# One conditioned attention block on one core: projections spread over the head slots, q and k side by side in one stack, six transfers per half stack in place of nine

## What is computed

```python
ln = (h - mu) / jnp.sqrt(var + EPS) * ln_g + ln_b
gamma = (w @ Wg.T + bg)[:, None, :]
beta = (w @ Wb.T + bb)[:, None, :]
# h = gamma * ln + beta
qkv = (h @ Wqkv.T + bqkv).reshape(B, N, num_heads, hd, 3)
energy = jnp.einsum('bhqd,bhkd->bhqk', q, k)
att = jax.nn.softmax(energy, axis=-1) / D ** 0.5
out = jnp.einsum('bhqk,bhkd->bhqd', att, v)
out = out @ Wp.T + bp
h1 = out + hidden
h2 = _sln(h1, w, ln_g, ln_b, Wg, bg, Wb, bb)
# result: h2 + h1
```

## Time and profile before

| what | value |
|---|---|
| median of 3 runs | 434.63 us (433.49 to 435.28) |
| profiled execution | 434.07 us |
| its span on the core, first to last instruction | 432.3 us |
| granted TensorE clock, mean | 0.963 |
| TensorE matmul busy | 376.3 us, 87% |
| VectorE busy | 316.9 us, 73% |
| ScalarE busy | 247.4 us, 57% |
| GpSimd busy | 44.4 us, 10% |
| DMA | 53.69 MB, mean 124 GB/s |

### The profile page before, as it was taken

One profiled execution on the slowest core, in us unless ns is written; L12 is line 12 of the kernel. 1 busy time (PEld: TensorE's weight loads), 2 busy tenths in 40 slices (PEclk: granted clock), 3 DMA queues, 4 the chain that ended last, 5 costly groups with the idle time before them and its releaser, 6 DMA issues.

```text
span 432.3 us, 9025 instructions
## 1 busy us (share of the span) xinstructions
PE 376.3 (87%) x3240; PEld 307.0 (71%) x3241; DVE 316.9 (73%) x777; ACT 247.4 (57%) x453; POOL 44.4 (10%) x46
## 2 busy tenths in 40 slices
PE   4958598899898999999998999898999999988972
PEld 4627496788686878877786878777877778766652
DVE  7617566669686887879797878787787978685644
ACT  7421247556474756566565757575656656664650
POOL 5000000002010100102020101010010201010111
PEclk9987779999899999999999999999999999999996
DMA  6198887878759668989697988779897978493021
GB/s 192 38 117 107 123 103 116 160 109 137 123 127 131 144 124 157 127 143 148 118 159 121 155 116 161 126 156 125 146 127 133 142 106 163 77 186 96 7 71 49
DMA packets 50367, 53.69 MB, mean 124 GB/s; under 512 B 6642, under 2 KB 41857, under 8 KB 50322
## 3 DMA queue, kind: packets, MB, share of 16 engines
q1 hardware_dynamic: 50322, 53.11, 73.6%
HBM read 14.18 MB, written 4.23 MB: 43 GB/s over the span
## 4 chain that ended last, share of the span: by engine, by line
PE 55%; DMA 14%; SPq 12%; issue 7%; DVE 7%; ACT 3%; POOL 0%; POOLq 0%; DVEq 0%; ACTq 0%
PE m L669 20%; DMA kst<-qk_l 14%; PE st L669 11%; PE sa L669 10%; SPq L286 10%; PE pv L669 10%; DVE mx L458 3%; PE pv L759 2%; SPq L289 2%; ACT p L436 2%; PE m L833 1%; ACT hT L424 1%; DVE qst L615 1%; DVE qk_l L492 1%; DVE m_l L467 1%
## 5 line engine op out<-in xcount | busy, mean ns | idle before, releaser
L458 DVE TENSOR_REDUCE mx<-sa 128x2 f32<-128x512 f32 x256 | 174.4, 683 | 93.5 <-PE sa L669 93.3
L436 ACT ACTIVATE p<-st 128x512 f32<-128x512 f32 x256 | 150.3, 598 | 78.3 <-PE st L669 75.0
L669 PE MATMUL sa<-kst,qst 128*128 128x256 f32 x512 | 109.8, 298 | 15.9 <-DMA kst<-qk_l 14.7
L669 PE MATMUL st<-qst,kst 128*128 128x256 f32 x512 | 111.4, 301 | 4.9 <-ACT p L436 4.9
L669 PEld LDWEIGHTS sa<-kst,qst 128*128 128x128 f32 x512 | 82.0, 198 | 21.7 <-DMA kst<-qk_l 13.3
L669 PEld LDWEIGHTS st<-qst,kst 128*128 128x128 f32 x512 | 79.4, 193 | 16.6 <-ACT p L436 9.4
L669 PE MATMUL pv<-p,v_st 128*32 128x256 f32 x1024 | 68.7, 386 | 0.7 <-ACT p L436 0.7
L349 POOL TENSOR_TENSOR h1b<-h,gb 128x512 f32<-128x512 f32 x16 | 20.4, 1277 | 250.4 <-DVE h L548 250.4
L669 PEld LDWEIGHTS pv<-p,v_st 128*32 128x32 f32 x1024 | 26.8, 109 | 20.5 <-ACT p L436 0.9
L669 PE MATMUL m<-hT_h,wqkv_h 128*128 128x256 f32 x128 | 39.0, 305 | 0.0
L669 PE MATMUL m<-hT_l,wqkv_h 128*128 128x256 f32 x128 | 37.5, 293 | 0.0
(11 more groups left out here) (97 smaller groups left out, 529.7 us busy)
## 6 DMA issues: line engine op xcount, KB each, us to landing
qst<-qk_h SPq DMA_DIRECT2D x64, 128.0 KB
qst<-qk_l SPq DMA_DIRECT2D x64, 128.0 KB
kst<-qk_h SPq DMA_DIRECT2D x64, 128.0 KB
kst<-qk_l SPq DMA_DIRECT2D x64, 128.0 KB
xa<-x_dram SPq DMA_DIRECT2D x16, 256.0 KB, 4.1
xd<-x_dram SPq DMA_DIRECT2D x16, 256.0 KB, 4.5
gb<-gb_rows SPq DMA_DIRECT2D x16, 256.0 KB, 4.5
out_dram<-y SPq DMA_DIRECT2D x16, 256.0 KB, 4.3
```

Source lines behind the costliest of these rows:

```text
L436: nc.scalar.activation(p32[:, h % PR, :], st_ps[h % 2][:], ACT.Exp).then_inc(exp_done, 1)
L458: dve.tensor_reduce(mx[:, par(a), h // HH, (h % HH) * TT:(h % HH + 1) * TT], sa_ps[h % 2][:].rearrange("p (t n) -> p t n", t=TT), AX.X, AL ...
L669: return nc.tensor.matmul(o, l, r, start=start, stop=stop)
```

## The change

- q and k lie side by side: `qk` holds for each half and part (high, low) q and then k, and one stack `qkst` of 67 rows has for each head q's 256 columns and then k's 256. Rows 0-15 (high of both) and 48-63 (low of both) are filled by one transfer of 256 KiB each, the others by four of 128 KiB. Six transfers for nine. The two whole halves wait for q's and k's low parts together.
- Row 64 is zero for q and stays so; `scores_max` multiplies only rows 0 to 64, `scores` all 67. So the rows of the maxima need no clearing, and no pad rows exist; the four large memsets at the start go.
- The projections' slots are lists: q in slots 0, 1, 3, 4, k in 1, 3, 4, 5, v in 7, 7, 8, 9, output in 11, 12, 13, 15. The transposes of x move from slot 13 to 11, the attention transposes to bank pv1, the maxima to pv0 (slot 1) and pv1 (slot 10), each with two transposes, since a maxima tile now has 8 rows of 256.
- h's high part is made from h in SBUF by one instruction, two slots after the transposes of x; its low part, the normalised x, and the bias of the output (now added to x before the residual, not by two matmuls) are GpSimd's.
- The table of VectorE follows; `residual` begins one step later.

```diff
-ROWS = 4 * HD + 2
+ZERO_ROW = 4 * HD
+ROWS = ZERO_ROW + 3
 VC = 2 * HD
 LAG = 3
 LEAD = 1
 PR = 8
 
-S_MT1, S_Q, S_K, S_MT0, S_AT, S_V, S_P, S_XT = 1, 2, 3, 7, 8, 8, 10, 13
+Q_SLOTS, K_SLOTS, V_SLOTS, P_SLOTS = (0, 1, 3, 4), (1, 3, 4, 5), (7, 7, 8, 9), (11, 12, 13, 15)
+S_MT1, S_AT, S_MT0, S_XT = 1, 8, 10, 11
+S_QH, S_KH, S_VH = 5, 6, 10
 WARM = 14
-NSTK = 9
+NSTK = 6
 S_O1, S_O0 = 3, 11
+S_OT1, S_OT0 = 5, 13
...
-        qk_h = sb("qk_h", [P, 2, 2, 2, N], F32R)
-        qk_l = sb("qk_l", [P, 2, 2, 2, N], F32R)
-        qst = sb("qst", [P, 2, H, N], F32R)
-        kst = sb("kst", [P, 2, H, N], F32R)
+        qk = sb("qk", [P, 2, 2, 2, 2, N], F32R)
+        qkst = sb("qkst", [ROWS, 2, H, 2, N], F32R)
         v_st = sb("v_st", [P, 2, TT, H, VC])
-        mx = sb("mx", [P, 2, 2, P])
-        m_h = sb("m_h", [HH * TT, 2, P], F32R)
-        m_l = sb("m_l", [HH * TT, 2, P], F32R)
+        mx = sb("mx", [P, 2, 2, TT, P])
+        m_h = sb("m_h", [HH, 2, N], F32R)
+        m_l = sb("m_l", [HH, 2, N], F32R)
...
+            for r in range(ZERO_ROW, ROWS):
+                sp.dma_start(raw(qkst[r:r + 1, :, :, 1, :]).rearrange("a p h n -> a (p h) n"),
+                             ones[0:2 * H, :]).then_inc(fixed_rows_in, 16)
+            sp.dma_start(raw(qkst[ZERO_ROW:ZERO_ROW + 1, :, :, 0, :]).rearrange("a p h n -> a (p h) n"),
+                         zrows[:]).then_inc(fixed_rows_in, 16)
...
-            def stack(a, g, t):
-
-                if not has(a):
-                    return
-                if first(a):
-                    sp.wait_ge(pad_v_zero, 1)
+            def stack(a, g):
+
+                if not has(a):
+                    return
                 wait(sp, st_done, 16 * (a - 2) + HH * (g + 1))
-                wait(sp, (ql_ready, kl_ready)[t], 1 * a + 1)
+                wait(sp, ql_ready, 1 * a + 1)
+                wait(sp, kl_ready, 1 * a + 1)
                 s, p = stack_in[g][par(a)], par(a)
-                dst, hi, lo = (qst, kst)[t], qk_h[:, p, t, g, :], qk_l[:, p, t, g, :]
-                for r, src in enumerate((hi, lo, hi, lo) if t == 0 else (hi, hi, lo, lo)):
-                    sp.dma_start(raw(dst[r * HD:(r + 1) * HD, p, g * HH:(g + 1) * HH, :]),
+
+                def part(r, t, src):
+                    sp.dma_start(raw(qkst[r * HD:(r + 1) * HD, p, g * HH:(g + 1) * HH, t, :]),
                                  raw(src)).then_inc(s, 16)
-                if t == 0:
-                    sp.dma_start(raw(qst[4 * HD:ROWS, p, g * HH:(g + 1) * HH, :]), zrows[:]).then_inc(s, 16)
+
+                for r, e in ((0, 0), (3, 1)):
+                    part(r, slice(0, 2), qk[:, p, g, e])
+                part(1, 0, qk[:, p, g, 1, 0])
+                part(1, 1, qk[:, p, g, 0, 1])
+                part(2, 0, qk[:, p, g, 0, 0])
+                part(2, 1, qk[:, p, g, 1, 1])
...
             def step(b):
-                stack(b + 1, 1, 0)
-                stack(b + 1, 1, 1)
+                stack(b + 1, 1)
                 maxima(b, 1)
                 if has(b + 4):
                     wait(sp, xn_ready, 1 * (b + 2) + 1)
                     sp.dma_start(xa[:, par(b + 4)], x_t[b + 4]).then_inc(x_in[par(b + 4)], 16)
-                stack(b + 2, 0, 0)
+                stack(b + 2, 0)
                 maxima(b + 1, 0)
-                stack(b + 2, 0, 1)
...
+            def norm_x(a):
+
+                wait(pool, rstd_ready, 1 * a + 1)
+                wait(pool, xnT_done, 1 * a)
+                for t in range(TT):
+                    o = pool.tensor_scalar(xn[:, t, :], xa[:, par(a), t, :], mv[:, t, 0:1], rstd[:, 0, t:t + 1],
+                                           ALU.subtract, ALU.mult)
+                o.then_inc(xn_ready, 1)
+
+            def add_bias(a):
+
+                if first(a):
+                    pool.wait_ge(bias_ready, 1)
+                wait(pool, xd_in[par(a)], 32 * (half(a) + 1))
+                pool.tensor_tensor(xd[:, par(a)], xd[:, par(a)],
+                                   bias_b[:].rearrange("p (a n) -> p a n", a=1).broadcast_to([P, TT, D]),
+                                   ALU.add).then_inc(xdb_ready, 1)
+
+            def low_h(a):
+
+                if not has(a):
+                    return
+                wait(pool, hTh_ready, 1 * a + 1)
+                pool.tensor_tensor(hT_l[:, par(a)], hT[:], hT_h[:, par(a)], ALU.subtract).then_inc(hTl_ready, 1)
+
...
+                    if h == 5 and has(b + 3) and not first(b + 3):
+                        norm_x(b + 3)
+                    if h == 9 and has(b - 1):
+                        add_bias(b - 1)
+                    if h == 13:
+                        low_h(b + 3)
...
-            def high_h(a, k):
-
-                if not has(a):
-                    return
-                wait(act, xnT_done, 1 * a + 1)
+            def high_h(a):
+
+                if not has(a):
+                    return
+                wait(act, hT_ready, 1 * a + 1)
                 wait(act, v_done, 1 * (a - 2) + 1)
-                nc.scalar.activation(hT_h[:, par(a), k, :], m0[:, k * N:(k + 1) * N], ACT.Identity,
-                                     bias=bcol[:, k:k + 1], scale=gcol[:, k:k + 1]).then_inc(hTh_ready, 1)
+                nc.scalar.activation(hT_h[:, par(a)], hT[:], ACT.Copy).then_inc(hTh_ready, 1)
...
-                    if h == S_Q + 4 and has(b + 2):
+                    if h == S_QH and has(b + 2):
...
-                    if h == S_K + 4 and has(b + 2):
+                    if h == S_KH and has(b + 2):
...
-                    if h == S_V + 4 and has(b + 1):
+                    if h == S_VH and has(b + 1):
...
-                    if h == 15:
-                        high_h(b + 3, 0)
-                        high_h(b + 3, 1)
+                    if h == S_XT + 2:
+                        high_h(b + 3)
...
-            act.wait_ge(consts_ready, 1)
-            for pad in (kst, qst):
-                nc.scalar.activation(pad[:, 1].rearrange("p h n -> p (h n)"),
-                                     ones[:, 0:1].broadcast_to([P, H * N]), ACT.Copy, scale=0.0).then_inc(pad_1_zero, 1)
...
-                dve.tensor_reduce(mx[:, par(a), h // HH, (h % HH) * TT:(h % HH + 1) * TT],
+                dve.tensor_reduce(mx[:, par(a), h // HH, :, h % HH],
...
-                    wait(dve, xd_in[par(a)], 32 * (half(a) + 1))
+                    wait(dve, xdb_ready, 1 * a + 1)
...
                 between = {
-                    (0, 0): [lambda: residual(b - 2, 2)],
-                    (0, 1): [lambda: low_h(b + 2), lambda: residual(b - 2, 3)],
-                    (2, 0): [lambda: norm1(b + 3, 0), lambda: low_max(b, 1)],
-                    (2, 1): [lambda: norm1(b + 3, 1)],
-                    (4, 0): [lambda: residual(b - 2, 4), lambda: norm1(b + 3, 2)],
-                    (5, 0): [lambda: normalise(b - 1, 1, 0)],
-                    (5, 1): [lambda: normalise(b - 1, 1, 1)],
-                    (6, 1): [lambda: low_qk(b + 2, 0, m0, qh_ready, ql_ready)],
-                    (7, 1): [lambda: low_qk(b + 2, 1, m1, kh_ready, kl_ready)],
-                    (8, 1): [lambda: low_max(b + 1, 0), lambda: residual(b - 2, 5)],
+                    (0, 0): [lambda: residual(b - 2, 0)],
+                    (1, 0): [lambda: residual(b - 2, 1)],
+                    (2, 0): [lambda: residual(b - 2, 2)],
+                    (2, 1): [lambda: low_max(b, 1)],
+                    (3, 0): [lambda: residual(b - 2, 3), lambda: norm1(b + 3, 0)],
+                    (3, 1): [lambda: norm1(b + 3, 1)],
+                    (4, 1): [lambda: norm1(b + 3, 2)],
+                    (5, 1): [lambda: low_qk(b + 2, 0, m0, qh_ready, ql_ready)],
+                    (6, 0): [lambda: normalise(b - 1, 1, 0)],
+                    (6, 1): [lambda: low_qk(b + 2, 1, m1, kh_ready, kl_ready)],
+                    (7, 0): [lambda: normalise(b - 1, 1, 1)],
+                    (8, 1): [lambda: residual(b - 2, 4)],
                     (9, 1): [lambda: low_att(b - 1)],
-                    (11, 0): [lambda: norm1(b + 3, 3)],
-                    (11, 1): [lambda: norm1(b + 3, 4)],
-                    (13, 0): [lambda: normalise(b, 0, 0)],
-                    (13, 1): [lambda: normalise(b, 0, 1)],
-                    (14, 1): [lambda: residual(b - 1, 0)],
-                    (15, 0): [lambda: residual(b - 1, 1)],
+                    (10, 1): [lambda: residual(b - 2, 5), lambda: norm1(b + 3, 4)],
+                    (11, 1): [lambda: low_max(b + 1, 0)],
+                    (14, 0): [lambda: normalise(b, 0, 0)],
+                    (14, 1): [lambda: normalise(b, 0, 1)],
                 }
...
-                          aT_l[:, k, t * P:(t + 1) * P], wp_h[:, k, :], wp_l[:, k, :], k,
-                          (ones_r[:, 0:P], rows[:, 2 * D:3 * D]))
+                          aT_l[:, k, t * P:(t + 1) * P], wp_h[:, k, :], wp_l[:, k, :], k)
...
-                    o = mm(sa_ps[h % 2][:, t * N:(t + 1) * N], qst[:, p, h, t * P:(t + 1) * P],
```

(71 more changed lines are left out.)

94 lines of the change are left out of this document (36 added, 58 removed).

## The result

| | before | after |
|---|---|---|
| median of its runs, us | 434.25 (4) | 451.41 (4; 449.90 to 452.37) |
| profiled run: span | 432.3 | 450.6 |
| mean granted TensorE clock, of 2.4 GHz | 0.963 | 0.899 |

A forecast was written before the change was run, and what follows sets the result against it. It took TensorE's matmuls plus waits for stack transfers as the bound: steps from 23.53 to 22.0 us save 18.4, step 1 2.0, start 1.5, step 14 0.7, end 0.3; 22.9 off 434.07 gives 411 us (407 to 416).

The forecast's parts named there:

- the rate of the stacks: Half-stack transfers, SBUF to SBUF: 127 GB/s assumed, so D, the data time, is 8.3 us; bounds 102 and 369 GB/s.
- rival 2: Stack transfers slow down when neighbouring blocks stop taking turns between row groups: D 9.5 us, 421 us (417 to 430), chance 0.17.
- The time of a half stack: First issue to landing of a half stack: 11.0 us less 0.13, less part of the lag, between 8.9 and 10.9.
- with shorter stalls I expect none: TensorE's clock: two steps partly at half clock after a stall, some 3 us of the 18.4 gained, would not recur.
- Rival 3: Stack queue slower still, at 102 GB/s: D 10.3 us, step 24.4 us, total 447 us, chance 0.07.
- Step without stack waits: One batch element on TensorE without DMA waits: 23.2 - 1.25 - 0.5 = 21.4 us.
- Step with them: One batch element with about 0.3 us of stack wait at each of two places: 22.0 us, between 21.4 and 22.9.
- Half of the lag goes with the zeros: Landing of a half stack: half of its 2.0 us lag was taken to go with the small transfer of zeros.
- The wait for k costs nothing: Second half stack now waits for k's low part before q goes too: no cost, ready with slot 7's scores.
- Set-up -1.5: Start of the run: first stack issued at 23.2 us, third half landing at 50.6, up to 54; 1.5 us gained.
- Rival 1: TensorE bounds, as the lag was the zeros' or longer runs are faster: step 21.4 us, total 403, chance 0.30.
- Rival 4: New waits eat the old ones, D about 10: nothing measurable, 434 us, chance 0.04.

The follow-up runs named there:

- order and rows mended: Changed kernel with eight 128 KiB blocks in the earlier kernel's order and score matmuls over 126 and 128 rows: 412.61 us, ratio 0.953.
- experiment 6: Rows and clock: the kernel before with score matmuls on 66 rows for 128, 442.78 us against 433.04; changed kernel, order restored, on 126 and 128 rows, 412.61 us.
- The version without such waits: Changed kernel without the low-against-low product, six blocks at rows 0, 16 and 64, matmuls over 126 and 128 rows: 390.22 us, ratio 0.902.
- experiment 1: Two kernels with DMAs only, half stacks moved in various orders: 10.7 us in before's order, 11.5 in after's, 12.3 with rows 0 and 32 in turn.
- the phase of four blocks: Part of the DMA-only kernels: only four 128 KiB blocks, all to rows 0 to 15, took 7.1 us.
- experiment 4: Changed kernel with eight single blocks in before's order, k's low part waited for only after q's four blocks: 419.89 us, for 420.32 with the joint wait.
- eight blocks in before's order: Changed kernel with each half stack sent as eight 128 KiB blocks in the earlier kernel's order, all else kept: 420.32 us against 433.10, ratio 0.969.
- the phases with a load of x: Part of the DMA-only kernels: a 256 KiB load of x ahead of a half stack; after's order cost 1.0 us more than before's.

## Why the prediction was wrong, by its own steps

**The step that failed is the rate of the stacks.** The text took D = 8.3 us at 127 GB/s, "the rows of the same kind", with 102 GB/s as the lower end. Those rows are of blocks that took turns, which the change ended. At the 109 GB/s of after's full windows D is 9.6, near rival 2's 9.5, in the mechanism that rival 2 named. "Nothing in the trace shows two such blocks in a row" was held against that rival; it was no evidence, since no row could have shown it.

**The time of a half stack was wrong by two terms.** It took 11.5 us from issue to landing, where the sum had 9.9. Only some 0.6 of the 1.6 us is the rate (before took 11.0, less 0.13 for the zeros). The other 1.0 is the half of the lag that was to go and stayed. By the text's own numbers 9.9 would have fitted into the 10.25 and 10.65 us that there were, without a wait; the 0.3 of wait at each place was the middle of its bounds and not worked out. The lag alone did not break the forecast: with order and rows mended a half stack still takes 10.9 us (first issue at 240.65, landing at 251.53), and the step 21.7 us, under the 22.0.

**Rival 2 then priced it too low** (421, which belongs to the lower end, 22.8, of its own step; 23.3 gives some 427). Its sum had waits alone. The second failed step is "with shorter stalls I expect none" of the half clock: the stalls got longer, 1.20 to 2.00 us, each of the 13 had 3.4 us at half clock behind it, or more, and the projections of q and k, which the next half stack needs, lie just there. In size it is as large as the first: a step took 2.2 us more than forecast, the waits in it 0.9 more (1.5 for 0.6), and 3.4 us at half clock cost up to 1.7 (an estimate, from TensorE's half speed). The reading under the forecast was wrong too: of the two long steps of before, only one has half clock. In the other the wait for the stack was longer, 1.08 us for 0.44, and TensorE kept its clock (timeline of TensorE and a stretch of 2 us, before):

```profile
136.57 0.51 PE L669 MATMUL sa<-kst,qst 128*128 128x256 f32 x2 [1.08 <-DMA kst<-qk_l]
```

```profile
140.00:142.00 2.00, 2.00 (x26) 1.39 (x25) 1.62 (x3) 1.20 (x2) 0.00 (x0) 1.00 0.28 35
```

Rival 3 came nearest in time (447), by luck: it wanted DMA engines that never rest, and they rested in each step while the queue waited for k's low part (share 0.00 in the window from 217).

**A cost that had no step at all:** the diff has 65 and 67 rows for 128, and the text did not ask what that does. For the duration of one matmul it does nothing (two score matmuls take 0.24 us at full clock in after too); for the clock it does. By experiment 6 it is worth 9.7 us in before, and 7.3 in the changed kernel (ratios 0.969 and 0.953, of 434).

**The account.** After's 451 becomes 0.969 x 434 = 421 with the order mended, and 413 with the rows mended too. The forecast was 411. That these agree is in part chance, since the sum had the lag too low and the step without waits too high.

Point by point:
- *Step without stack waits*: 21.4 forecast. The version without such waits ran at 20.7, with 20.1 of slots. Of the 1.3 us of gaps that the text kept, half went too.
- *Step with them*: 22.0 forecast; 24.2 after, 21.7 with order and rows mended. The time from issue to need was right: 10.25 forecast for the half wanted in slot 15, and 228.89 - 1.36 - 217.37 = 10.2 in after.
- *Half of the lag goes with the zeros*: wrong. The small transfer cost 0.2 us (experiment 1). In the phase of four blocks, which has none, the data had passed by 85.2 us (4 GB/s in the window from 85 to 86) and the landing is at 86.8, 1.6 us later.
- *The wait for k costs nothing*: right (experiment 4).
- *No wait for the exponential, for k's low part, or for h's low part from GpSimd*: right, but for the two short waits for an exponential, in the first and last steps.
- *Set-up -1.5*: wrong in after. The third half stack landed with the scores at 58.52, against 54.3. From the first issue that is 34.0 us, where before took 32.2 and eight blocks in before's order 31.5: the low rate is worth some 2.5. The first issue was at 24.53 and not at 23.2, for a reason that the text had no step for: TensorE stood idle for 2.41 us until 14.53, for the load of the output weights. The version with eight blocks had no such wait in its profiled run, issued at 20.43 and had its third half stack at 51.92, within the forecast's 50.6 to 54 by luck; why the load landed in time there no run explains.
- *Step 1, 24.0 to 22.0*: 105.28 less the slot 14 before it, 78.71, is 26.6. *Step 14, -0.7*: 2.8 more. Step 1 has the wait in slot 15 (2.73) and 6.8 us at half clock; step 14 has 2.00 in slot 15 and 1.60 in slot 7. *End, -0.3*: 30.2 us from slot 14 of step 14 to the end, before 30.3.
- *Loads ahead of a half stack push it by 0.2 to 0.5*: 0.5 to 0.7 in the phases with a load of x (11.41 and 11.25 against 10.75 and 10.74).
- *Rival 1* (403) rested on the lag or on faster 2 KiB runs. Neither is so. Rival 4 (434) is not what was measured either.

## What to carry to other kernels

A DMA rate read from a trace belongs to the order of destinations that made it. When a change reorders the blocks of a queue, compare the rows of neighbours, and let blocks that lie 32 rows apart not follow each other. Where a transfer sits in a loop with TensorE, look whether half clock follows its waits, and price both: here it followed every wait with 65 rows in after, and some with more rows. And before cutting the rows of a matmul to what holds data, look at the granted clock: zero rows cost no time in any step here, and where TensorE had waits they kept the clock up.

## What the runs showed of the hardware

- The granted clock depends on the rows that the score matmuls cover. With the same transfers it was 0.529 at 49 and 51 rows and 0.966 at 65 and 67; with the waits of before 0.930 at 66 rows and 0.963 at 128. A TensorE without a gap was held at 1.2 GHz for nearly a whole run. Nothing between 51 and 65 rows was tried, and why rows count stays open.
- Blocks of 128 KiB, SBUF to SBUF into 16 rows: 100 GB/s if all go to one row group, or in turn to two that are 32 rows apart; some 125 if they differ otherwise. Four groups in turn (0, 16, 64, 80) were no faster than two. What sets the 125 is open.
- The landing lags the last data by some 2.0 us in before, and by 1.6 in the transfers alone (the phase of four blocks). A small transfer at the end or in between moves the landing by 0.2 us.
